# A transformer block on one core: the first batch's normalisation, modulation and weight splitting are reordered

## The reference

```python
mod = (_silu(L0_c) @ L0_wmod).reshape(8, 6, 1, -1)
sa, ca, ga, sb, cb, gb = (mod[:, 0], mod[:, 1], mod[:, 2], mod[:, 3], mod[:, 4], mod[:, 5])
ga = (2 * (ga >= 0) - 1) * jnp.maximum(jnp.abs(ga), 0.25)      # gb likewise
h = _layernorm(x) * (1 + ca) + sa
attn = softmax((h * w_lhs) @ (h * w_rhs).T) @ h                # per batch
x = x + ga * attn
h = _layernorm(x) * (1 + cb) + sb
x = x + gb * (relu(h @ W1 + b1) @ W2 + b2)
```

## Time and profile before

| | |
|---|---|
| median of 3 runs | 760.05 us (759.6 to 760.21) |
| the profiled execution: its own time | 759.2 us |
| the profiled execution: its span, first to last instruction | 757.4 us |
| TensorE busy | 739.7 us, 98% |
| VectorE / ScalarE / GpSimd busy | 556.1 / 402.1 / 377.9 us |
| mean granted TensorE clock | 0.988 |

### The profile page before, as it was taken

The page is one execution under the profiler, slowest core; times in us unless marked ns, Lnnn a source line. Parts: engine busy times, 40 slices in busy tenths (PEclk is TensorE's granted clock), DMA queues, the critical chain, the costliest instruction groups (busy, mean ns, idle before and its releaser), DMA issues.

```text
span 757.4 us, 13855 instructions
## 1 busy us (share of the span) xinstructions
PE 739.7 (98%) x4949; PEld 676.1 (89%) x4949; DVE 556.1 (73%) x981; ACT 402.1 (53%) x565; POOL 377.9 (50%) x388
## 2 busy tenths in 40 slices
PE   7789999999999999999999999999999999999997
PEld 6468899998999989999999989999899998999887
DVE  3769688975979758995789859797588957775511
ACT  2215438762487435873377733874358633754443
POOL 4543437453556527565275534655364661635543
PEclk7899999999999999999999999999999999999999
DMA  7010110102110020102101021100211021000100
GB/s 278 1 51 0 50 36 29 57 1 77 62 52 3 27 81 30 55 0 76 35 28 55 0 76 37 52 29 1 77 60 55 0 76 36 1 29 1 36 29 29
DMA packets 30680, 32.35 MB, mean 43 GB/s; under 512 B 2176, under 2 KB 28864, under 8 KB 30656
## 3 DMA queue, kind: packets, MB, share of 16 engines
q1 hardware_dynamic: 30656, 32.04, 12.9%
HBM read 23.61 MB, written 8.42 MB: 42 GB/s over the span
## 4 chain that ended last, share of the span: by engine, by line
PE 93%; DVE 4%; issue 1%; POOL 1%; ACT 1%; SPq 0%; DMA 0%; DVEq 0%
PE acc L388 8%; PE acc L383 8%; PE acc L382 8%; PE col L439 8%; PE col L441 8%; PE col L440 8%; PE score L508 7%; PE score L511 7%; PE score L507 7%; PE score L426 4%; PE score L425 4%; PE score L424 4%; PE col L482 3%; PE score L430 3%; PE score L500 2%; PE score L422 2%
## 5 line engine op out<-in xcount | busy, mean ns | idle before, releaser
L838 POOL TENSOR_TENSOR hid_lo<-hid,hid_hi 128x512 fp32r<-128x512 f32 x128 | 179.7, 1409 | 241.1 <-ACT hid_hi L538 239.6
L534 ACT ACTIVATE hid<-col,b1T 128x512 f32<-128x512 f32 x128 | 86.9, 679 | 113.5 <-PE col L441 113.0
L382 PE MATMUL acc<-W2hi,hid_hi 128*128 128x256 f32 x512 | 128.6, 283 | 0.0
L383 PE MATMUL acc<-W2lo,hid_hi 128*128 128x256 f32 x512 | 128.3, 282 | 0.0
L671 DVE TENSOR_SCALAR_CACHE_REDUCE S<-score 128x1024 f32<-128x1024 f32 x64 | 77.6, 1220 | 63.7 <-PE score L430 40.7
L538 ACT ACTIVATE hid_hi<-hid 128x512 fp32r<-128x512 f32 x128 | 81.0, 633 | 59.0 <-PE acc L388 56.5
L507 PE MATMUL score<-V,Phi 128*128 128x258 f32 x448 | 111.3, 284 | 0.0
L508 PE MATMUL score<-V,Phi 128*128 128x256 f32 x448 | 109.8, 283 | 0.0
L439 PE MATMUL col<-h2hi,W1hi 128*128 128x512 f32 x256 | 102.8, 402 | 0.7 <-ACT featT L550 0.7
L441 PE MATMUL col<-h2hi,W1lo 128*128 128x512 f32 x256 | 100.9, 394 | 0.0
L440 PE MATMUL col<-h2lo,W1hi 128*128 128x512 f32 x256 | 100.9, 394 | 0.0
(11 more groups left out here) (106 smaller groups left out, 1450.5 us busy)
## 6 DMA issues: line engine op xcount, KB each, us to landing
x_cur<-x SPq DMA_DIRECT2D x16, 512.0 KB, 3.3
ln<-x SPq DMA_DIRECT2D x14, 512.0 KB, 3.5
out<-x_mlp SPq DMA_DIRECT2D x8, 512.0 KB, 3.0
out<-x_mlp SPq DMA_DIRECT2D x16, 256.0 KB, 2.4
W_sb<-W SPq DMA_DIRECT2D x2, 1024.0 KB, 9.6
attn_mod<-mod_rows SPq DMA_DIRECT2D x8, 256.0 KB, 3.4
x_mlp<-wmod SPq DMA_DIRECT2D x1, 1024.0 KB, 7.1
gb_b<-mod_rows SPq DMA_DIRECT2D x8, 128.0 KB, 3.3
```

The source lines that it names most:

```text
L382: nc.tensor.matmul(o, hi, W2hi[:, it, :], start=(it == 0 and t % 2 == 0), stop=False, skip_group_check=True)
L383: nc.tensor.matmul(o, hi, W2lo[:, it, :], start=False, stop=False, skip_group_check=True)
L534: nc.scalar.activation(hid[:, n % 2, :], col[cb][:], ACT.Relu, bias=b1T[:, n % FT:n % FT + 1]).then_inc(col_read, 1)
L838: G.tensor_tensor(hid_lo[:, n % RING, :], hid[:, n % 2, :], hid_hi[:, n % RING, :].bitcast(F32), ALU.subtract).then_inc(hid_lo_done, 1)
```

## The change

Six edits, all in what comes ahead of the first batch's last scores:

- N0 of both halves is shared: VectorE takes the first two tiles, GpSimd the other two. Both add the negated mean `nm1` instead of subtracting `mv1`.
- The four products of MF become four steps. MF.0 and MF.1 stand between T0.0 and T0.1, with a filler matmul after each pair; MF.2 is ahead of SC.0 and MF.3 behind it. MA's products get such fillers too, and the runs of fillers change (13 ahead of MA, 2 behind, none behind T0.0). SA stands behind T0.1.
- On VectorE the read of SC.0 comes ahead of MF, and the next batch's L1.0 behind SC.1.
- On GpSimd WS moves behind XC, and it is cut into eight instructions of 512 elements. The wait for `w_ready` moves from MB to T2.0.
- T0 uses `col` for half 0 and `score[1]` for half 1, and T0.1 waits until the modulation there has been read.
- x's first half is loaded ahead of cT.

```diff
     "pe": """
-        MA.0+ T0.0+ SA.0+ T0.1+
+        MA.0+ T0.0+ MF.0+ MF.1+ T0.1+ SA.0+
...
-        SI.0+ L1.0+ L1.1+ T0.0+ N0.1+ T0.1+
+        SI.0+ L1.0+ N0.0+ L1.1+ T0.0+ N0.1+ T0.1+
...
+            def modulation_by_feature(part, modT, spare):
+
+                for k in range(DK):
+                    for kk in range(DK):
+                        last = nc.tensor.matmul(modT[:, k * NB:(k + 1) * NB], wmod_part(kk, part, k * P, P), siluT[:, kk, :],
+                                                start=(kk == 0), stop=(kk == DK - 1))
+                    keep_busy(spare)
+                return last
...
-                        keep_busy(12)
+                        keep_busy(13)
...
-                        modulation_by_feature((1, 0), mod_a_ps)
-                        keep_busy(4)
+                        for at, m in enumerate((1, 0)):
+                            last = modulation_by_feature(m, mod_a_ps[:, at * DK * NB:(at + 1) * DK * NB], 1)
+                        last.then_inc(modT_mm, 1)
+                        keep_busy(2)
...
                         pe.wait_ge(v_first[n], HT)
+                        if n == 1:
+                            pe.wait_ge(modT_ready, 2)
...
-                        if n == 0:
-                            keep_busy(6)
...
-                        for i in range(n * HT, (n + 1) * HT):
-                            V_.tensor_scalar(V_first[:, i, 0:D], x_cur[:, i, :], mv1[:, i, 0:1], rs1[:, i:i + 1], ALU.subtract, ALU.mult).then_inc(v_first[n], 1)
+                        for i in range(n * HT, n * HT + 2):
+                            V_.tensor_scalar(V_first[:, i, 0:D], x_cur[:, i, :], nm1[:, i:i + 1], rs1[:, i:i + 1], ALU.add, ALU.mult).then_inc(v_first[n], 1)
...
-                            G.tensor_tensor(lo[:], both, hi[:].bitcast(F32), ALU.subtract).then_inc(w_ready, 1)
+                            chunk = lo.shape[1] // 2
+                            for c in range(0, lo.shape[1], chunk):
+                                for half in range(2):
+                                    cols = slice(half * lo.shape[2] // 2, (half + 1) * lo.shape[2] // 2)
+                                    last = G.tensor_tensor(lo[:, c:c + chunk, cols], both[:, c:c + chunk, cols], hi[:, c:c + chunk, cols].bitcast(F32), ALU.subtract)
+                            last.then_inc(w_ready, 1)
```

More of the change, by code:

```diff
@@ L59 @@
     "dve": """
-        SI.0+ L1.0+ L1.1+ T0.0+ N0.1+ T0.1+
+        SI.0+ L1.0+ N0.0+ L1.1+ T0.0+ N0.1+ T0.1+
     """,
     "pool": """
-        L1.0+ N0.0+ L1.1+
+        L1.0+ N0.0+ L1.1+ N0.1+
     """,
@@ L71 @@
     "pe": """
-        MF.0 SC.0 SC.1 SC.2 MD.0 SC.3 SC.4 SC.5 SC.6 SC.7 MB.0 TH.0+ AV.0 AV.1 AV.2 AV.3 AV.4 TH.1+ AV.5
-        T2.0 AV.6 AV.7
+        MF.2 SC.0 MF.3 SC.1 SC.2 MD.0 SC.3 SC.4 SC.5 SC.6 SC.7 MB.0 TH.0+ AV.0 AV.1 AV.2 AV.3 AV.4 TH.1+
+        AV.5 T2.0 AV.6 AV.7
     """,
@@ L78 @@
     "dve": """
-        MF.0 SC.0 L1.0+ SC.1 SC.2 GA.0 SC.3 SC.4 SC.5 SC.6 SC.7 SB.0 SB.1 SB.2 SB.3 L1.1+ AV.0 SB.4 AV.1
+        SC.0 MF.0 SC.1 L1.0+ SC.2 GA.0 SC.3 SC.4 SC.5 SC.6 SC.7 SB.0 SB.1 SB.2 SB.3 L1.1+ AV.0 SB.4 AV.1
         SB.5 TH.0+ AV.2 SB.6 AV.3 SB.7 AV.4 TH.1+ AV.5 T2.0 AV.6 AV.7 VO.0 XG.0 XG.1
@@ L82 @@
     "pool": """
-        WS.0 L1.0+ N1.0+ XC.0 XC.1 XC.2 XC.3 L1.1+ N1.1+ L2.0 N2.0 L2.1
+        L1.0+ N1.0+ XC.0 XC.1 XC.2 XC.3 WS.0 L1.1+ N1.1+ L2.0 N2.0 L2.1
     """,
@@ L171, in block_kernel @@
         mod_a, mod_b = sb("mod_a", [P, 2 * DK]), sb("mod_b", [P, 2 * DK])
-        mod_l, mod_r = sb("mod_l", [P, 2 * DK]), sb("mod_r", [P, 2 * DK])
         attn_mod, gb_b2, gb_all = sb("attn_mod", [P, 2, D]), sb("gb_b2", [P, D]), sb("gb_all", [P, D])
@@ L199, in block_kernel @@
         inv_sum = sb("inv_sum", [P, 1])
+        mod_l, mod_r = sb("mod_l", [P, 2 * DK]), sb("mod_r", [P, 2 * DK])
         wmod_a = S[:, 7, :].rearrange("p (k n) -> p k n", k=DK)
@@ L222, in block_kernel @@
         max_ps = score[1]
-        featT_ps = [[acc[:, kk, :, :].rearrange("p a d -> p (a d)") for kk in range(DK)], [col[0][:], col[1][:]]]
+        featT_ps = [[col[0][:], col[1][:]], [score[1][:, 0:HR], score[1][:, HR:ROWS]]]
         av_ps = [score[0][:, 0:VW], score[0][:, HR:HR + VW]]
@@ L285, in _ @@
             wmod_rows = wmod.rearrange("(k p) n -> p k n", p=P)
+            sp.dma_start(x_cur[:, 0:HT, :], x_rows[0, 0]).then_inc(x_in[0], 16)
             sp.dma_start(cT_sb, cT.rearrange("(k p) b -> p k b", p=P)).then_inc(c_in, 16)
-            sp.dma_start(x_cur[:, 0:HT, :], x_rows[0, 0]).then_inc(x_in[0], 16)
             sp.dma_start(wmod_a, wmod_rows[:, :, 0:2 * D]).then_inc(wmod_a_in, 16)
@@ L348, in wmod_part @@
                 return staged[:, kk, at + start:at + start + width]
[L350 to L358, removed]
             def keep_busy(count):
@@ L467, in part @@
                         pe.wait_ge(wmod_b_in, 16)
-                        modulation_by_feature((4, 3, 2, 5), mod_b_ps)
+                        last = modulation_by_feature((4, 3, 2, 5)[n], mod_b_ps[:, n * DK * NB:(n + 1) * DK * NB], 1 if ph is PH["before"] else 0)
+                        if n == 3:
+                            last.then_inc(modT_mm, 1)
                     elif kind == "MD":
@@ L476, in part @@
                         else:
+                            if ph is PH["first"]:
+                                pe.wait_ge(w_ready, 2)
                             pe.wait_ge(ln2_done, 2 * (b if n == 0 else f) + n + 1)
@@ L484, in part @@
                     elif kind == "MB":
-                        if ph is PH["first"]:
-                            pe.wait_ge(w_ready, 2)
                         pe.wait_ge(scores_read, T * b + T)
@@ L847, in part @@
                         pool.wait_ge(ln1_rstd, n + 1)
-                        for i in range(n * HT, (n + 1) * HT):
-                            G.tensor_scalar(V_first[:, i, 0:D], x_cur[:, i, :], mv1[:, i, 0:1], rs1[:, i:i + 1], ALU.subtract, ALU.mult).then_inc(v_first[n], 1)
+                        for i in range(n * HT + 2, (n + 1) * HT):
+                            G.tensor_scalar(V_first[:, i, 0:D], x_cur[:, i, :], nm1[:, i:i + 1], rs1[:, i:i + 1], ALU.add, ALU.mult).then_inc(v_first[n], 1)
                     elif kind == "WS":
```

## The result

The changed kernel takes 742.23 us (median of 4 runs, 742.14 to 743.54) against 759.83 us: ratio 0.9775, 95% interval 0.9758 to 0.9792. Span of the profiled execution 740.3 us instead of 757.4, granted clock 1.000 instead of 0.988.

What follows compares the result with a forecast made beforehand. TensorE is almost always busy from 56 us, so the first attention product's start, delayed by waits and VectorE's stall, decides. Gains 3.75 + 0.75 + 0.75 + 4.28 + 1.55 = 11.1, less 1.2, give 9.9: 760.05 to 750.1 us, range 747.4 to 754.0.

Steps and rivals of the forecast that it cites:

- allowance for the clock: First stage on TensorE: one 2.5 us stretch at half clock, 1.2 us taken off the gain, bounds 0 and 4.
- T0.1 earlier: Second half's first transposes on TensorE: start at 16.3 instead of 20.04 us, 3.75 us gained.
- T0.1 to SC.0: TensorE up to the first scores: 3.6 us instead of 4.36, since fewer narrow passes stand there; 0.75 gained.
- SC.0 to SC.1's transposes, with VectorE's stall: First two score tiles: 5.9 instead of 6.67 us, 0.75 gained, and TensorE's 4.28 us wait for VectorE goes.
- SC.2: Third score tile on TensorE: 3.2 us instead of 4.77 at half clock, 1.55 gained.
- SC.3 to AV.0: From the end of SC.2 to the first attention product: order as before, 14.7 us, no gain.
- the change touches only the short stretch: Only the time before the first attention product, up to 56 us, was to change; no gain counted after it.
- The normalisation: First batch's N0, shared by GpSimd and VectorE: 1.8 us per half, one engine after another; range 1.1 to 3.1.
- The stall: VectorE's modulation, held up by GpSimd's weight subtraction: finished near 24.7 us, so TensorE's 4.28 us wait goes.
- The load order: x loaded ahead of cT at the start: cT lands later, so VectorE's statistics start 0.4 us late.
- The weights' subtraction behind XC: GpSimd's eight pieces, 41 to 51 us: costed at nothing, with 7 us of cover before TH.1.
- Rival C: The change frees more: no exclusion, cT in time, full clock; gain 12.7 us, 747.3; chance 0.05.

Runs made afterwards that it cites:

- b_layout: Kernel before with only mod_l and mod_r allocated last, so activations lie 64 bytes lower; 754.40 us, ratio 0.9929.
- a_layout_back: Changed kernel with mod_l and mod_r allocated behind mod_b again, restoring the addresses of before; 746.29 us, ratio 0.9826.
- a_nofill: Changed kernel without the filler matmuls between the narrow products; 745.22 us, ratio 0.9806.
- a_mf_block: Changed kernel with the four modulation steps in one block ahead of SC.0, without fillers; 743.98 us.
- a_ws_early8: Changed kernel with the eight pieces of the weights' subtraction back at the old place, ahead of the next batch's L1.0; 749.77 us.
- a_whole_w64: Changed kernel with the weights' subtraction uncut, weights 64 bytes higher and activations at their old places; 741.00 us, ratio 0.9753.
- b_ws_late: Kernel before with GpSimd's two whole weight subtractions moved behind XC, and T2.0 waiting for them instead of MB; 752.63 us, ratio 0.9918.
- a_ws_whole: Changed kernel with the weights' subtraction in two instructions instead of eight, at the new place behind XC; 741.20 us, ratio 0.9781.
- b_ws8: Kernel before with GpSimd's weights' subtraction cut into eight at its old place; 754.26 us.

## Why the prediction was wrong

The direction and the place were right, the size not: 9.9 forecast, 17.1 in the profiled pair of spans. Of the 7.2 us between them 3.6 lie behind AV.0, 1.8 in T0.1, 1.2 in the allowance for the clock and 0.6 in the rest. By its own steps:

| step | forecast | measured |
|---|---|---|
| T0.1 earlier | 3.75 | 5.58 (20.04 to 14.46) |
| T0.1 to SC.0 | 0.75 | 0.90 |
| SC.0 to SC.1's transposes, with VectorE's stall | 5.03 | 5.25 |
| SC.2 | 1.55 | 1.75 |
| allowance for the clock | -1.2 | 0 |
| SC.3 to AV.0 | 0 | 0.06 |
| behind AV.0 | 0 | 3.56 |

- **What failed first is the sentence that the change touches only the short stretch.** The sum ended at AV.0. The changed allocation of `mod_l` and `mod_r` was in the change and got no term; b_layout and a_layout_back show that its addresses alone give 3.9 and 4.0 us behind AV.0 (703.09 against 699.05 in the second; up to 5 against the kernels with the shortest rest). Without it the median would be 746.3 (a_layout_back), 1.1 us below the range; so this alone doesn't make it right.
- **The normalisation was under-sized.** Taken one after another at 1.8 us, the shared tiles took 1.3 (8.75 to 10.08): VectorE's 0.415 and 0.579, GpSimd's 0.687 and 0.579, against 0.408 and 0.558 alone. They slow each other but don't exclude each other for their whole length. This is shown for one-input instructions on both sides only. Beside GpSimd's two-input instructions the same form on VectorE is held up, in the changed kernel too, where three of these four tiles take 1.16 to 1.37 us against 0.40 alone and each ends 0.15 us after GpSimd's instruction:

```profile
95.27 1.46 POOL L841 TENSOR_TENSOR hid_lo<-hid,hid_hi 128x512 fp32r<-128x512 f32 x1 [3.66 <-ACT hid_hi L541]
95.71 4.07 DVE L791 TENSOR_SCALAR ln<-x_cur,nm,rs 128x256 f32<-128x256 f32 x4
96.68 2.62 POOL L888 TENSOR_TENSOR x_cur<-x_cur,attn_mod 128x512 f32<-128x512 f32 x2
```

The long cases of L788 in the earlier trace rows, on which the prediction built its turn-taking, all stand beside such two-input instructions, so they said nothing of this pairing. And the prediction let VectorE's statistics of half 1 wait for all of it; they stand behind VectorE's own share only and started at 9.58 instead of 10.9.
- **The clock** was mis-sized for this pair: 1.2 us were taken off for a fall that didn't come. Without the fillers it comes and costs 4.3 (a_nofill). With them it comes in some profiles all the same (a_mf_block, a_ws_early8, a_whole_w64), and in a_whole_w64 AV.0 is then 1.2 late, the size that was allowed. So the 0 in the table is in part luck.
- **The stall** was right, in place, cause and size, with L644 and L648 at 0.18 us. Its removal alone moves AV.0 by 7.0, part of it through the clock (b_ws_late).
- **SC.2**: the prediction's 3.2 us are less than its own terms (2.75 and five times 0.13 make 3.4); 3.02 were measured.
- **The load order:** ScalarE began on cT at 4.38, and the statistics began at 5.21, 0.08 late instead of 0.4. In the other profiles with this order they begin at 5.27 to 5.57, so the 0.4 lay within what the landings vary.
- **The weights' subtraction behind XC** at no cost was right: AV.0 and the products behind it don't wait for it. The cut there has no benefit (a_ws_whole).

Rival C was the nearest (747.3), and for its reasons (no exclusion, full clock).

## What to carry to other kernels

Read a diff for its allocations too: moving two tiles of 16 bytes was worth about 4 us here, nearly a quarter of the whole gain. When one engine's long instruction blocks another's tiny ones, move it to where nothing of the kind runs; after cutting it, a blocked step still waits for a piece, three of them in b_ws8 and six in a_ws_early8. And look at the granted clock around narrow matmuls instead of assuming it: without fillers between them at the start the clock fell and cost 4.3 us (a_nofill), while 32 of them in one block later on left it at 1.00 (a_mf_block).

## What the runs showed of the hardware that was not expected

- TensorE's time per pass depends on where its operands lie to each other in SBUF: 88.9 us per batch with the addresses of before, 88.38 with the activations 64 bytes lower, 88.2 with the weights 64 higher, 88.83 with the activations 64 higher, 88.74 with them 128 higher.
- GpSimd's normalisation of a 128x256 tile takes 1.222 us with `mv1` subtracted and 0.558 with `nm1` added.
- VectorE's normalisation of such a tile takes 0.415 and 0.579 us beside GpSimd's one-input form, but 1.37 when it starts beside a two-input instruction of GpSimd (0.40 alone).
- In a_nofill the clock is at 0.50 from 8.2 to 21.9 us, though TensorE is busy in the microseconds shown above; 1.29 us of waiting and eight-column passes came before the fall. Four such passes and two filler passes in turn went with 1.00 in the changed kernel's profile, but not in each: in a_whole_w64's it fell once, from 10.2 to 13.6 us. In a_mf_block 32 eight-column passes in a row, from 18.22 us on, left it at 1.00.
